# Two-layer adaLN block: the routing front between attention and experts, rearranged over the engines

## The reference, cut to what matters

```python
mod = (_silu(L0_c) @ L0_wmod).reshape(L0_c.shape[0], 6, 1, -1)
sa, ca, ga, sb, cb, gb = (mod[:, 0], mod[:, 1], mod[:, 2], mod[:, 3], mod[:, 4], mod[:, 5])
ga, gb = ...                                   # magnitude at least 0.25
h = _layernorm(x, axis=-1) * (1 + ca) + sa
x = x + ga * _L0_attn_ref(h, Wq, Wk, Wv, Wo, bo)
h = _layernorm(x, axis=-1) * (1 + cb) + sb     # <- the layer norm that the change is about
x = x + gb * _L0_ffn_ref(h, gate_w, gate_proj_w, up_proj_w, down_proj_w)
# _L0_ffn_ref: logits = h @ gate_w.T; softmax; top 2, weights renormalised;
#   out = sum over the token's two experts e of w_e * down_e(silu(gate_e h) * up_e h)
# then layer 1 with its own six modulation vectors, in the same two steps
```

## Time and profile before

| | |
|---|---|
| median of 3 runs | 2007.04 us (2003.31 to 2009.59) |
| profiled execution, whole time | 2002.69 us |
| its span, first to last instruction | 2000.9 us |
| mean granted TensorE clock, share of 2.4 GHz | 0.953 |
| PE busy | 1842.2 us (92%), 8492 matmuls |
| DVE busy | 1191.6 us (60%) |
| ACT busy | 716.7 us (36%) |
| POOL busy | 686.3 us (34%) |
| DMA | 218.46 MB, mean 109 GB/s |

### The profile page before, as it was taken

The page is one execution under the profiler, slowest core; times in us unless marked ns, Lnnn a source line. Parts: engine busy times, 40 slices in busy tenths (PEclk is TensorE's granted clock), DMA queues, the critical chain, the costliest instruction groups (busy, mean ns, idle before and its releaser), DMA issues. The chain is left out here.

```text
span 2000.9 us, 25863 instructions
## 1 busy us (share of the span) xinstructions
PE 1842.2 (92%) x8492; PEld 1450.2 (72%) x8492; DVE 1191.6 (60%) x2112; ACT 716.7 (36%) x1369; POOL 686.3 (34%) x697
## 2 busy tenths in 40 slices
PE   8989999999999999998457898989889999999996
PEld 5657888888888888876356676657768778787784
DVE  4557666666666666677853343647465747566664
ACT  2434454445444444433112232355523122213220
POOL 1435121212112222111353555533344445435442
PEclk9999999999999999998758998988999999999998
DMA  6221454435353525421375999610001011101011
GB/s 237 79 71 60 138 159 130 152 95 164 90 189 105 189 82 186 126 85 37 106 258 162 334 267 261 159 52 11 27 27 42 17 32 48 31 5 53 6 53 42
DMA packets 101122, 218.46 MB, mean 109 GB/s; under 512 B 8640, under 2 KB 33232, under 8 KB 99504
## 3 DMA queue, kind: packets, MB, share of 16 engines
q1 hardware_dynamic: 78848, 168.70, 26.0%
q0 software_dynamic: 11584, 28.97, 6.1%
q10 hardware_dynamic: 10608, 19.74, 3.1%
HBM read 126.02 MB, written 91.37 MB: 109 GB/s over the span
## 5 line engine op out<-in xcount | busy, mean ns | idle before, releaser
L744 PE MATMUL bank<-hT,W1b 128*128 128x512 f32 x512 | 208.9, 408 | 14.8 <-DVE hh L1989 14.8
L1743 DVE RECIPROCAL rr<-rr 128x256 f32<-128x256 f32 x128 | 218.8, 1730 | 4.7 <-ACT num L1212 4.7
L744 PE MATMUL bank<-W1a,hT 128*128 128x512 f32 x512 | 209.7, 410 | 3.4 <-DVE hT L1657 3.4
L745 PE MATMUL bank<-hT,W1b 128*128 128x512 f32 x512 | 204.0, 399 | 0.0
L746 PE MATMUL bank<-hT,W1b 128*128 128x512 f32 x512 | 203.6, 398 | 0.0
L746 PE MATMUL bank<-W1a,hT 128*128 128x512 f32 x512 | 202.0, 395 | 0.0
L745 PE MATMUL bank<-W1a,hT 128*128 128x512 f32 x512 | 201.2, 393 | 0.0
L2115 POOL TENSOR_TENSOR x<-x,tmp 128x512 f32<-128x512 f32 x64 | 101.3, 1583 | 272.2 <-DVE tmp L1735 272.2
L1989 DVE TENSOR_TENSOR hh<-hh,bank 128x512 f32<-128x512 f32 x64 | 43.4, 686 | 195.4 <-PE bank L746 166.0
L1762 DVE SCALAR_TENSOR_TENSOR kt<-bank,kt 128x256 fp32r<-128x256 f32 x128 | 50.8, 397 | 173.9 <-ACT vt L1228 173.7
L2053 POOL TENSOR_TENSOR W<-stage,W 128x1024 fp32r<-128x1024 f32 x32 | 76.9, 2404 | 189.5 <-ACT W L1131 187.2
(11 more groups left out here) (274 smaller groups left out, 4644.0 us busy)
## 6 DMA issues: line engine op xcount, KB each, us to landing
hs_d<-bor SPq DMA_DIRECT2D x24, 1548.0 KB, 11.3
ws_d<-W SPq DMA_DIRECT2D x48, 512.0 KB, 6.3
WB<-ws_d SPq DMA_DIRECT2D x8, 3072.0 KB, 17.9
stage<-wa SPq DMA_DIRECT2D x32, 512.0 KB, 5.3
stage<-wbe SPq DMA_DIRECT2D x24, 512.0 KB, 4.2
stage<-wdn SPq DMA_DIRECT2D x24, 512.0 KB, 3.9
mw<-wmod SPq DMA_DIRECT2D x10, 1024.0 KB, 5.0
hg<-hs_d ACTq DMA_DIRECT2D x39, 258.0 KB, 5.7
```

The lines of the kernel that those rows point to most:

```text
L744: pe.matmul(o, lhs(HI), rhs(HI), start=start, stop=False, **kw)
L745: pe.matmul(o, lhs(HI), rhs(LO), start=False, stop=False, **kw)
L1743: dve.reciprocal(rr[:, pair, h], rr[:, pair, h]).then_inc(r_rec, 1)
```

## The change

Layer norm of the expert block (k=1):
- ScalarE normalises. VectorE still makes the statistics, then `row_scales`, with one more small operation (minus mean times rstd, into `nmean`). `ln_rows` on ScalarE writes x times rstd plus nmean, four activations. `apply_rows` and `mrow_load` are gone.
- Modulation is applied per partition behind the transposes: ScalarE's copy to `hF` takes scale and bias from `modc[:, 1]`. So (0, SB) and (0, CB) become columns: two more "col" entries in A0 b0 and A0 b1, two row stores less, three operations of GpSimd less.
- The scattered rows must hold the modulated values, so `hF` is transposed back: `rows_back` on TensorE, 16 transposes a batch in four ring entries ("hb"), `rows_out` on ScalarE, four copies a batch into `hb[b]`.
- `need_h(1, b)` waits for `ring_read` in place of `ring_done`; ScalarE's copies for k=1 no longer wait for `ring_done`; the scatter no longer waits for the rows' own semaphore.

Order: in `front` the last step's statistics, inversion and output halves are interleaved anew, `LAST_A` stands behind router(2), and prefix(1) right behind it.

```diff
-COL_KIND = {(0, SA): 0, (0, CA): 1, (1, SA): 0, (1, CA): 1, (1, SB): 2, (1, CB): 3}
+COL_KIND = {(0, SA): 0, (0, CA): 1, (0, SB): 2, (0, CB): 3, (1, SA): 0, (1, CA): 1, (1, SB): 2, (1, CB): 3}
-MOD_FINISH = [(0, 1, 2), (3,), (4,), (9,)]
+MOD_FINISH = [(0,), (3,), (4,), (9,)]
-ROUTES = [("rt", 0), ("pf", 0)]
-FRONT = [("rt", 1), ("tail", *LAST_A), ("ln", 1, 2, 0), ("ln", 1, 2, 1), ("pf", 1), ("rt", 2),
-         ("ln", 1, 3, 0), ("ln", 1, 3, 1), ("pf", 2), ("rt", 3), ("pf", 3)]
+ROUTES = [("rt", 0), ("hb", 0, 0), ("hb", 0, 1), ("pf", 0)]
+FRONT = [("rt", 1), ("ln", 1, 2, 0), ("ln", 1, 2, 1), ("hb", 1, 0), ("hb", 1, 1), ("rt", 2), ("tail", *LAST_A),
+         ("pf", 1), ("hb", 2, 0), ("hb", 2, 1), ("ln", 1, 3, 0), ("ln", 1, 3, 1), ("pf", 2), ("rt", 3),
+         ("hb", 3, 0), ("hb", 3, 1), ("pf", 3)]
...
# SyncE: mrow_load(b) and its four calls
-                for k, kind in enumerate((R_CB0, R_SB0)):
-                    sp.dma_start(mrow[:, k, :], rows_d[kind, b, :].partition_broadcast(P)).then_inc(bmrow_full, 16)
...
# TensorE
-                pe.wait_ge(ring_done, ln_end(k, b))
+                pe.wait_ge(ring_read if k == 1 else ring_done, ln_end(k, b))
+
+            def rows_back(b, half):
+
+                need_h(1, b)
+                for i in range(2):
+                    n, t = RING[("hb", b, half)] + i, 2 * half + i
+                    o = ring_slot(n, n % 2)
+                    for c in range(NC):
+                        last = pe.transpose(o[:, c * P:(c + 1) * P], hF[:, c, b * S + t * P:b * S + (t + 1) * P], ident[:, :])
+                    last.then_inc(ring_full, 1)
...
+                    if routing and t >= 2:
+                        rows_back(0, t - 2)
...
# ScalarE, ln_out
-                        act.activation(hF[:, c, b * S:(b + 1) * S], TAIL[n % 2][:, :], ACT.Copy) \
+                        act.activation(hF[:, c, b * S:(b + 1) * S], TAIL[n % 2][:, :], ACT.Identity,
+                                       scale=modc[:, 1, 1, c, b:b + 1], bias=modc[:, 1, 0, c, b:b + 1]) \
...
+            def ln_rows(b):
+
+                act.wait_ge(ln_scales, b + 1)
...
+                for t in range(NT):
+                    last = act.activation(xn_of(1, b)[:, t, :], x[:, b * NT + t, :], ACT.Identity,
+                                          scale=rstd[:, t:t + 1], bias=nmean[:, t:t + 1])
+                last.then_inc(xn_ready, 1)
+
+            def rows_out(b, half):
+
+                n0 = RING[("hb", b, half)]
+                act.wait_ge(ring_read, n0)
+                for i in range(2):
+                    act.wait_ge(ring_full, n0 + i + 1)
+                    act.activation(xn_of(1, b)[:, 2 * half + i, :], TAIL[(n0 + i) % 2][:, :], ACT.Copy) \
+                        .then_inc(ring_read, 1)
...
# ScalarE, step_a: the rows stand between the output halves and the queries
                     out_hi(s, 1)
+                if ln and not first:
+                    ln_rows(ln[1])
...
# ScalarE, front
                 num_out(NB * GA - 1, 1)
-                for pair in range(2):
-                    out_hi(NB * GA, pair)
+                ln_rows(2)
+                out_hi(NB * GA, 0)
                 router(1)
                 ln_out((1, 2), 0)
+                out_hi(NB * GA, 1)
                 ln_out((1, 2), 1)
+                rows_out(1, 0)
+                rows_out(1, 1)
                 router(2)
+                rows_out(2, 0)
+                rows_out(2, 1)
+                ln_rows(3)
                 ln_out((1, 3), 0)
                 ln_out((1, 3), 1)
                 router(3)
+                rows_out(3, 0)
+                rows_out(3, 1)
...
# VectorE
+            def row_scales(b):
+
+                if b > 0:
+                    dve.wait_ge(xn_ready, ln_index(1, b))
+                ln_rstd()
+                dve.scalar_tensor_tensor(out=nmean[:, :], in0=mv[:, :, 0], scalar=-1.0, in1=rstd[:, :],
+                                         op0=ALU.mult, op1=ALU.mult).then_inc(ln_scales, 1)
...
# VectorE, choice: now also writes the token numbers
+                dve.wait_ge(xn_ready, ln_index(1, b) + 1)
...
# VectorE, step_a
-                if routing:
-                    choice(0)
                 if tail_of("A", g, b):
                     out_lo(s, 0)
                     out_lo(s, 1)
-                if ln and not first:
-                    ln_apply(*ln)
+                if routing:
+                    choice(0)
...
# VectorE, front
-                for pair in range(2):
-                    invert(NB * GA, pair)
-                    normalise(NB * GA, pair)
-                for pair in range(2):
-                    out_lo(NB * GA, pair)
+                stats((1, 2), range(NT))
+                invert(NB * GA, 0)
+                normalise(NB * GA, 0)
                 logits(1)
-                stats((1, 2), range(NT))
-                ln_apply(1, 2)
+                invert(NB * GA, 1)
+                normalise(NB * GA, 1)
+                out_lo(NB * GA, 0)
+                out_lo(NB * GA, 1)
                 choice(1)
+                logits(2)
                 for t in range(NT):
                     tail_evac("front", 0, 0, t)
+                positions(1)
                 stats((1, 3), range(NT))
-                positions(1)
-                ln_apply(1, 3)
-                logits(2)
                 choice(2)
                 positions(2)
                 logits(3)
...
# GpSimd, front
                 passed(RING[("rt", 1)])
-                add_tail(LAST_A, RING[("tail", *LAST_A)])
                 ln_out((1, 2), 0)
                 ln_out((1, 2), 1)
+                passed_rows(1)
+                passed(RING[("rt", 2)])
+                add_tail(LAST_A, RING[("tail", *LAST_A)])
                 passed(RING[("pf", 1)])
                 scatter(1)
-                passed(RING[("rt", 2)])
+                passed_rows(2)
                 ln_out((1, 3), 0)
```

More of the change, by code:

```diff
@@ L1230, in step_a @@
                         .then_inc(pj_hi, 1)
+                    if b == 3 and last and t >= 2:
+                        rows_out(0, t - 2)
                 if b == 3 and last:
@@ L1697, in stats @@
                     ln_stats(*ln, tiles)
-                    if NT - 1 in tiles:
+                    if NT - 1 in tiles and ln[0] == 1:
+                        row_scales(ln[1])
+                    elif NT - 1 in tiles:
                         ln_rstd()
```

88 lines of the change are left out of this document (35 added, 53 removed).

## The result

The changed kernel takes 1992.51 us (median of 6 runs, 1988.15 to 1996.63) beside 2005.28 us for the kernel before on the same chip (6 runs, 2000.96 to 2010.10): ratio 0.9933, 95% interval 0.9911 to 0.9956. Measured a second time, with 6 more runs, it is 0.9942 (0.9928 to 0.9956). Of 2005 us that is a gain of 13.4 us (8.8 to 17.8), and of 11.6 (8.8 to 14.4) the second time; the prediction's sum was 10.1. The profiled execution took 1994.45 us with a span of 1992.7, so profile against profile the gain is only 8.2 us. Executions of one kernel lie 4 to 5 us to either side of their median, and a landmark of one profile says no more than that.

What follows compares the result with a forecast made beforehand. TensorE was taken to bound the kernel nearly throughout, but VectorE and engine hand-overs the front. Terms +1.5 −3.3 −4.0 +0.6 −4.9 = −10.1 us took the 2007.0 us median to 1996.9; range 1989 to 2005.

Steps and rivals of the forecast that it cites:

- two columns, up to A7 b1: First group, batches 0 and 1: two more modulation columns delay the row 2 product; +1.5 us, between +0.5 and +4.
- A7 b2: Group 7 batch 2: TensorE's 2.09 us wait before the transposes goes and the tail's clock stays up; −3.3 us.
- A7 b3: Group 7 batch 3: VectorE loses 5.5 us of rows, choice moves behind output halves, clock holds; −4.0 us.
- last product to tail's end: Front, last attention product to GpSimd's last addition: halt gone, but router(2) and four rows-back entries ahead of the tail; +0.6 us.
- tail's end to last scatters: Front behind the last tail: prefix(1) and positions(1) already done, chain to the last scatters 30.9 us, before 36.0; −4.9 us.
- last scatters to gather: Scatter landing until the slots' first row loads: the sum takes nothing for sharing DMA engines with expert loads; 0.
- The price is hidden under the wait of 2.29: Group 7 batch 3: extra transposes shrink TensorE's wait before the last key-value tile; without that cover, 3 us.
- Rival 2: Extra transposes and later copies leave TensorE at 1.2 GHz in group 7 batch 3; gain 4.3, 2002.7 us; chance 0.13.
- rival 1: Transposes and ScalarE's copies run in series, 2.1 us an entry for 1.1; all 18 entries give 2015 us; chance 0.08.
- the tail's own halt of 12 us is gone: Front, middle of the last tail: TensorE's 12.16 us wait for VectorE disappears, set against work put ahead; net +0.6 us.
- Rival 3: Scatters become the end: landing slows beside expert loads, the last may lose 6.2 us; gain 4, 2003 us; chance 0.12.
- Rival 4: Router(2) and router(3) run at the upper level, 3.7 us each; −6.6 us more, 1990 us; chance 0.10.

Runs made afterwards that it cites:

- experiment 3: The changed kernel without the 64 transposes of `rows_back` and ScalarE's 16 copies of them, rows left unmodulated; 1987.93 us, ratio 0.992.
- experiment 4: The changed kernel's engines and operations, with the front in the order before the change (last tail first, batch 2 statistics behind output halves); 1987.17 us, ratio 0.9912.
- the early tail: The changed kernel with the last tail right behind batch 2's forward transposes, ahead of router(2); 1984.50 us in experiment 5 and in experiment 9.
- experiment 5: The changed kernel with the last tail right behind batch 2's forward transposes, batch 3's rows ahead of router(2); 1984.50 us, ratio 0.9901.
- experiment 9: The kernel of experiment 5 with the first column's transposes behind modulation row 2's product in A0 b0; 1984.50 us, ratio 0.9898.
- experiment 10: The kernel of experiment 9 plus seven unread matmuls, four behind router(1) and three behind batch 2's forward transposes; 1983.82 us, ratio 0.9903.
- experiment 11: The kernel of experiment 9 with the second expert's weight load waiting for all scatters and the first three gathers; 1985.28 us, ratio 0.991.
- experiment 7: The changed kernel with 14 more matmuls in the front whose results nobody reads; 1987.93 us, ratio 0.9912.
- Experiment 6: The kernel of experiment 4 with the second expert's weights loaded only when all scatters have landed; one run, 1991.00 us.
- the column behind the row: The kernel of experiment 4 with the first column's transposes behind modulation row 2's product in A0 b0; 1984.66 us, ratio 0.9899.

## Why the prediction was right, and where not

The forecast of a gain held, and its sum of 10.1 us lies within the interval of the measured one (8.8 to 17.8). The median was forecast at 1996.9 and is 1992.51. Of these 4.4 us, 1.8 are the base, which was 2007.04 in three executions and is 2005.28 in six. Step by step, profiled execution against profiled execution:

| step | predicted | measured | again |
|---|---|---|---|
| two columns, up to A7 b1 | +1.5 | +3.1 | +1.7 |
| A7 b2 | −3.3 | −3.2 | −3.2 |
| A7 b3 | −4.0 | −5.0 | −5.1 |
| last product to tail's end | +0.6 | +1.2 | +1.2 |
| tail's end to last scatters | −4.9 | −5.2 | −5.1 |
| last scatters to gather | 0 | +0.7 | +0.3 |
| sum | −10.1 | −8.4 | −10.3 |

That the sum comes as close as −8.4 and −10.3 is partly luck. In the first profile the columns cost 1.6 us more than forecast, the way to the tail's end 0.6 and the landing 0.7, while A7 b3 gained 1.0 more; and whether the columns' 1.6 come is a matter of the execution.

- *Columns.* The place and the mechanism were right, +1.3 ahead of the row product. What was mis-sized is the clock behind it: 5.28 us for 3.59 in some executions. The reserve up to +4 held it.
- *A7 b2* came as worked out: up to the transposes it is 2.2 us shorter, which is the wait of the earlier trace rows, and from there to the product 1.0 shorter, the tail being at the upper level.
- *A7 b3.* Up to the end of the queries it is 1.4 us shorter, as worked out. "The price is hidden under the wait of 2.29": the wait is gone, and 0.8 us of the transposes remain by experiment 3. The mis-sized part is the way from the queries to the tail: 8.1 us before, measured from 949.84, where prefix(0) starts; forecast 5.5; in the new trace the queries end at about 948.3 and the tail begins at 953.10, so 4.8. Prefix(0) waited 1.55 us for the choice, not 2.2. The tail itself became 0.2 shorter. Rival 2, the clock falling there for good, did not come.
- *Product to tail's end.* Counted from the end of the last product (965.89; the forecast's 963.7 with the first group's 1.5 is 965.2), the chain ran as worked out up to the router: statistics 0.9 ahead of it, inversions 4.5 behind it, router(2) 18.5 behind it (forecast 18.8) and 6.97 long. The ring's last four entries went at 1.0 each (3.86 us), so rival 1 is out. The mis-sized term is the tail: 12.1 us (991.17 to 1003.27) for 10.9. Its parts as forecast, 2.8, twice 1.35, twice 1.95 and 1.3, add up to 10.7. Measured, VectorE gets the first tile after 3.1 us, and the second 2.35 after the first instead of 1.35, because it waits for TensorE, whose first groups of three are 1.28 to 1.43 us apart at the lower level. Then it is 1.4, 1.85 and 2.0, near enough as forecast.
- *What the sum did not ask* is whether the new place is a good one. Both its terms (six ring entries and router(2) ahead of the tail) were in the +0.6, set against "the tail's own halt of 12 us is gone". Their price is about 4 us up to the first gather by experiment 4 (83.3 and 83.0 us from the last product in the changed kernel, 78.8 with the order of before), and 5 to 9.5 against the early tail (73.8, 77.1, 78.3 and 77.5 in experiments 5, 9, 10 and 11). The halt is gone, but experiment 4 shows that this halt would have shrunk to 5.5 us by itself, as soon as the rows left VectorE's queue. The sum compared the new order with the old kernel, not with the old order on the new engines.
- *Tail's end to scatters.* 30.7 for 30.9; the terms as listed add up to 30.8, and from 36.0 that is −5.2, not the −4.9 of the sum. "Hidden, but only just" for rows_back(3) is right: prefix(3) waits 0.68 us for its last copy, which ends at 1029.97, as choice(3) does, and without the copies (experiment 3) the stretch is as long.
- *Rival 3* is real, but small in this kernel: 0.3 to 0.7 us, up to 4 in experiment 7. The sum took nothing for it by the row of an undisturbed landing. The Trainium skill, page "DMA: Bandwidth & Descriptors", section "Issuing engines are not separate DMA queues", says that DMAs started by different engines run on the same 16 DMA engines and interleave. Experiment 6 agrees: 3.0 us without the weights, 6.6 with them.
- *Rival 4* did not come: router(2) and router(3) both 6.97. The routers' speed was put down to idle time before them; experiment 7 shows that the clock also falls without it.

What stays open: the prediction wanted every stage behind the front as long as before. The gain of 8.4 us at the first slot's matmul had shrunk to 4.6 at the end of the slots in the first profile and was 8.2 at the end of the execution; in the second, 10.2 became 9.4. TensorE's largest waits in the slots of the first profile are 5.0, 4.3 and 5.7 us, of which the profile puts the last down to expert weights. Over all profiles the way from the first slot to the combined products is 220 to 228 us, in no order that follows the front (224.6 before, 228.4 and 225.5 changed, 228.2 and 222.8 in experiments 5 and 9). No run here took that stage apart. Against the changed kernel's 1992.5 us the order of before is 5.3 us faster by medians where its landmarks say 4.4, and with the column behind the row 7.8; the early tail is 8.0 faster (experiments 5 and 9) where its landmarks say 5 to 9.5. These agree within the 4 to 5 us of one profile, and no closer.

## What to carry over

When a change both takes work off an engine and moves work about, cost the old order with the new engines as well: the stall that the move is aimed at may go by itself. Look twice before putting something that one engine does alone (here a router that holds TensorE for 7 us) ahead of work on which two others wait. And look at what is on the DMA queues when the last small transfers of a stage start: here each microsecond closer to a load of 3 MB costs up to 0.7 us.

## What the runs showed of the chip

- The same eight matmuls behind the same wait of 0.95 us took 5.28 and 5.29 us in two profiles and 3.59 in six; behind router(0) the clock fell in 11 of the 14 profiles and not in three (44.7 or 42.9 us for the step in the kernels with rows back). The Trainium skill, page "TensorE: Matmul & The Clock Gate", section "Part 1: The HAM clock gate", says that one and the same kernel has a different number of matmuls at the lower level from run to run. The two profiles of the changed kernel agree: 5.28 in one, 3.59 in the other.
- 32 matmuls of 8 columns took 3.63 to 3.74 us at the upper level, 6.97 at the lower one, and 3.9 to 6.4 when the clock fell in between.
- A scatter of 128 rows landed in 3.0 us (median of the last eight) with no weights on the queues and 3.1 in the kernel before, in 5.3 and 6.4 with the last scatters 12.7 and 10.4 us behind the issue of a 3 MB load, in 8.0 with them 6.4 us behind it.
- Beside GpSimd's addition VectorE's multiplication with both inputs in SBUF takes 1.26 us instead of 0.69; with the 0.69 us of the operation before it this is the 1.9 us of the tail's last tiles.
